# A fused linear attention and expert layer on one core: another order of work, six groups in flight instead of five

## What is computed

```
h    = layer_norm_over_channels(x)
q, k, v = h Wq + bq, h Wkv + bkv                  # 8 heads of 16
Q, K = elu(q) + 1, elu(k) + 1
out[l] = Q[l] . sum_{m<=l} K[m] v[m]^T / (Q[l] . sum_{m<=l} K[m])    # per head
x1   = x + out
t    = layer_norm_over_channels(x1)
probs = softmax(t gate_w + router_gamma), the two largest of 8 kept -> c[e]
y    = x1 + sum_e c[e] * (gam[e] * (t expert_w[e] + expert_b[e]) + bet[e])
```

## Time and profile before

| what | us |
|---|---|
| median of 3 runs (lowest, highest) | 998.53 (997.16, 1003.74) |
| the profiled execution, its own time | 1006.48 |
| span of that execution, first to last instruction | 1004.8 |
| PE busy | 832.0 |
| DVE busy | 766.5 |
| ACT busy | 440.0 |
| POOL busy | 405.4 |

### The profile page before, as it was taken

How to read it: one execution, slowest core, us unless ns; L and a number is a source line. 1 busy time by engine, 2 the same in 40 slices (tenths; PEclk the granted TensorE clock), 3 DMA queues, 4 the chain that set the end, 5 groups by cost and what they waited for, 6 DMA issues and landing times.

```text
span 1004.8 us, 25364 instructions
## 1 busy us (share of the span) xinstructions
PE 832.0 (83%) x8137; PEld 689.0 (69%) x8137; DVE 766.5 (76%) x2550; ACT 440.0 (44%) x1297; POOL 405.4 (40%) x639
## 2 busy tenths in 40 slices
PE   4678888888988889888888888888888898888885
PEld 2556667776777677766777777776667776767764
DVE  4677777778778887887877787778787778788764
ACT  1234444444444444444444444444444444444333
POOL 3254334434344444344443443344444334444311
PEclk9789888989889998999988998899998989898888
DMA  3000000000000000000000000000000000000000
GB/s 90 11 12 1 22 23 22 23 21 21 21 21 21 21 21 21 21 21 21 21 13 8 21 21 21 21 21 21 21 21 21 21 21 21 21 23 11 12 12 21
DMA packets 41200, 20.76 MB, mean 21 GB/s; under 512 B 1584, under 2 KB 41168, under 8 KB 41168
## 3 DMA queue, kind: packets, MB, share of 16 engines
q1 hardware_dynamic: 41168, 20.35, 7.5%
HBM read 10.90 MB, written 9.44 MB: 20 GB/s over the span
## 4 chain that ended last, share of the span: by engine, by line
PE 43%; DVE 33%; issue 14%; ACT 7%; DVEq 1%; POOL 1%; DMA 0%; SPq 0%; ACTq 0%; POOLq 0%
PE big L833 8%; DVE probs L540 6%; PE bank_n L845 6%; PE bank_n L887 5%; PE big L865 4%; DVE hot L614 4%; DVE y_dve L652 4%; PE bank_n L947 4%; ACT y_act L371 3%; DVE qkv L547 3%; DVE bn L527 3%; PE big L867 3%; PE big L866 3%; DVE o L670 2%; PE bank_q L906 2%
## 5 line engine op out<-in xcount | busy, mean ns | idle before, releaser
L540 DVE TENSOR_TENSOR probs<-big,tri 128x512 f32<-128x512 f32 x288 | 195.9, 681 | 75.6 <-PE big L833 75.6
L371 ACT ACTIVATE y_act<-big,scale 128x128 f32<-128x128 f32 x576 | 163.7, 374 | 0.0
L285 POOL TENSOR_TENSOR ve<-mv,eps 128x4 f32<-128x4 f32 x72 | 14.7, 204 | 318.4 <-DVE mv L532 318.3
L865 PE MATMUL big<-e_high,x_high 128*128 128x512 f32 x288 | 130.9, 455 | 10.5 <-DVE probs L540 4.9
L833 PE MATMUL big<-q_t,k_even 32*128 32x128 f32 x1152 | 75.2, 333 | 69.5 <-DVE y_dve L652 66.8
L833 PEld LDWEIGHTS big<-q_t,k_even 32*128 32x128 f32 x1152 | 54.1, 217 | 92.1 <-issue 89.8
L866 PE MATMUL big<-e_low,x_high 128*128 128x512 f32 x288 | 114.2, 396 | 0.0
L867 PE MATMUL big<-e_high,x_low 128*128 128x512 f32 x288 | 114.1, 396 | 0.0
L547 DVE SCALAR_TENSOR_TENSOR qkv<-bank_p,rstd,b_qkv 128x384 f32<-128x384 f32 x72 | 44.1, 613 | 72.0 <-PE bank_p L854 72.0
L652 DVE SCALAR_TENSOR_TENSOR y_dve<-big,scale,y_dve 128x128 f32<-128x128 f32 x288 | 87.1, 344 | 2.5
L652 DVE SCALAR_TENSOR_TENSOR y_dve<-big,scale,y_one 128x128 f32<-128x128 f32 x144 | 49.1, 345 | 46.7 <-ACT y_one L366 46.7
(11 more groups left out here) (150 smaller groups left out, 2086.9 us busy)
## 6 DMA issues: line engine op xcount, KB each, us to landing
x<-in_x SPq DMA_DIRECT2D x36, 256.0 KB, 3.0
out<-o SPq DMA_DIRECT2D x36, 256.0 KB, 2.3
beta_raw<-in_L_ffn_beta_w SPq DMA_DIRECT2D x1, 512.0 KB
e_raw<-in_L_ffn_expert_w SPq DMA_DIRECT2D x1, 512.0 KB
w_raw<-in_L_conv_Wkv SPq DMA_DIRECT2D x2, 64.0 KB, 2.3
b_qkv<-in_L_conv_bkv SPq DMA_DIRECT2D x1, 128.0 KB, 4.7
w_raw<-in_L_conv_Wq SPq DMA_DIRECT2D x1, 64.0 KB, 2.6
b_qkv<-in_L_conv_bq SPq DMA_DIRECT2D x1, 64.0 KB, 3.6
```

The costliest lines, as they stand in the source:

```text
L371: last = nc.scalar.activation(y_act[:, c.par, u, e], big[2 * s][:, 128 * e:128 * e + 128], ACT.Copy, scale=scale[:, c.par, u, e:e + 1])
L540: tt(probs[:, half, g].rearrange("p u e t -> p (u e) t"), big[g][:].rearrange("p (n t) -> p n t", t=T), tri[:].unsqueeze(1).broadcast_to([ ...
L865: mm(big[bank][:], x1_high[:, c.par, u], e_high[:, w], start=True, stop=False)
```

## The change

Every engine's step is written anew. The arithmetic, the shapes and the number of PE, DVE and POOL operations for one group stay as they are; one copy on ACT goes.

- **Stages.** A step now has six groups in flight, `g[0]` to `g[5]`: in step k, `g[n]` is group k - n. The steps run from k = 0 to 40, 41 in all. g[0] is the load and the transpose of x, g[1] its statistics' second part and low part, g[2] the projections and features, g[3] the sums of k, the transposes of k and q, the second half of the scores and the new state, g[4] the first half of the scores, attention, x1 and the first part of the routing, g[5] the rest of the routing, the experts, the output and the store.
- **Order.** The operations of different stages are interleaved in a new order on every engine, written out by hand in `step(k, g)`.
- **PSUM.** The banks have no owners. `AT`, `PROJ_AT`, `SCORES_AT` and `EXPERTS_AT` say in which of the eight banks each product stands; a bank serves three or four of them in turn within a step. The two halves of a unit's experts are apart in the order, and both halves of unit 2 stand in bank 1, one after the other.
- **Semaphores.** Each operation has its own, which counts groups, so that every wait is "n + 1" or near it.
- **x_res.** ACT's copy is gone. SP loads the same part of x from HBM a second time, into `x_res`, two steps before it is added.
- **The rest.** `y_one` has four buffers instead of two. The products of the remaining weights (`rest_of_weights`), which stood behind the first projections, now stand ahead of them, at the start of step 2, with a wait for the DVE operations that read them.

The diff is long (it writes all the step functions anew), so here are the constants, the order of stages, SP, and the start of PE's step; where the rest of the order matters, rows of it are shown below.

```diff
+REST_PSUM = 2 + 6 + EXPERTS + 1
+LAGS = 6
+REST_STEP = 2
+AT = dict(x=4, kv=3, att=6, x1_a=6, x1_b=4, k=1, q=7, coef=0, out=1)
+PROJ_AT = (4, 0, 3, 2)
+SCORES_AT = ((3, 7, 2, 0), (0, 5, 6, 7))
+EXPERTS_AT = ((4, 2), (6, 5), (1, 1), (2, 3))
...
-        y_one = sb("y_one", [128, 2, 128])
+        y_one = sb("y_one", [128, U, 128])
...
-            first, last = 2, CHUNKS - 2
-            for k in range(-2, PAR * first):
-                step(grp(k + 2), grp(k + 1), grp(k), grp(k - 1), grp(k - 2))
...
+            first = (LAGS + PAR) // PAR + 1
+            for k in range(PAR * first):
+                step(k, [grp(k - n) for n in range(LAGS)])
+            with eng.Fori(first, CHUNKS) as t:
+                for j in range(PAR):
+                    step(None, [Group(moved(t, (j - n) // PAR), (j - n) % PAR) for n in range(LAGS)])
+            for k in range(GROUPS, GROUPS + LAGS - 1):
+                step(k, [grp(k - n) for n in range(LAGS)])
...
+                if g[0]:
+                    n, p = g[0].i, g[0].par
+                    need(sp, "x_turned", n - 1)
+                    need(sp, "x_low", n - 1)
+                    if k != 0:
+                        sp.dma_start(x[:, p], dram(x_d, p, at[0])).then_inc(x_loaded[p], 16)
+                if g[5]:
+                    n, p = g[5].i, g[5].par
+                    need(sp, "out", n + 1)
+                    sp.dma_start(dram(out_d, p, at[5]), o[:, p]).then_inc(stored[p], 16)
+                if g[2]:
+                    n, p = g[2].i, g[2].par
+                    need(sp, "x1", n - 1)
+                    sp.dma_start(x_res[:, p], dram(x_d, p, at[2])).then_inc(x_res_loaded[p], 16)
...
-                    nc.scalar.activation(x_res[:, a.par], x[:, a.par], ACT.Copy).then_inc(S["x_res_done"], 1)
...
+            def step(k, g):
+                if k == REST_STEP:
+                    rest_of_weights()
+                    pe.wait_ge(S["rest_dve"], REST_PSUM)
+                if k == REST_STEP + 1:
                     pe.wait_ge(S["rest_dve"], REST_DVE)
```

More of the change, by code:

```diff
@@ L47 @@
 REST_DVE = 2 + 6 + EXPERTS + 2 + 4
[L48 to L56, removed]
+REST_PSUM = 2 + 6 + EXPERTS + 1
[5 more added lines that the diff above has]
+EXPERTS_AT = ((4, 2), (6, 5), (1, 1), (2, 3))
+WEIGHTS_AT = (0, 1, 2, 3)
+FIRST_AT = WEIGHTS_AT[0]
 class Group:
@@ L168, in program @@
         o = sb("o", [128, PAR, U, T])
[L170 to L183, removed]
+        bank = [ps(f"bank{n}") for n in range(8)]
@@ L192, in need @@
         def need(eng, name, count):
[L194 removed]
+            if not isinstance(count, int):
                 eng.wait_ge(S[name], count)
[L197 to L198 removed]
+            elif count > 0:
+                eng.wait_ge(S[name], min(count, GROUPS))
         def steps(eng, step):
@@ new lines, in turn_x, with project, turn_k @@
+            def turn_x(p):
+                for u in range(U):
+                    last = transpose(x_units[u], x[:, p, u], ident[:])
+                return last
+            def project(p, u):
+                out = bank[PROJ_AT[u]][:, 0:384]
+                mm(out, x_high[:, p, u], w_high[:], start=True, stop=False)
+                mm(out, x_high[:, p, u], w_low[:], start=False, stop=False)
+                return mm(out, x_low[:, p, u], w_high[:], start=False, stop=True)
+            def turn_k(p):
+                for u in range(U):
+                    last = transpose(bank[AT["k"]][:, T * u:T * u + T], feat[:, p, u, 128:256], ident[:])
+                return last
@@ L827, in scores, with turn_q @@
+            def turn_q():
+                for u in range(U):
+                    last = transpose(bank[AT["q"]][:, T * u:T * u + T], qn[:, u], ident[:])
+                return last
+            def scores(p, half):
                 for v in range(HALF_U):
@@ new lines, in values, with key_values @@
+                        for i in range(PAIRS):
+                            last = mm(bank[AT["att"]][32 * i:32 * i + 32, T * u:T * u + T], v_pad[:, p, u, 2 * i + e],
+                                      probs[:, half, i, v, e], start=False, stop=(e == 1), skip_group_check=True)
+                return last
+            def key_values(p):
+                for u in range(U):
+                    last = mm(bank[AT["kv"]][:, 128 * u:128 * u + 128], feat[:, p, u, 128:256], qkv[:, p, u, 256:384],
+                              start=True, stop=True)
+                return last
```

1197 lines of the change are left out of this document (633 added, 564 removed), and 9 rows, old and new, of the table names.

## The result

The changed kernel takes 755.89 us (median of 4 runs, 753.64 to 757.29); the kernel before took 999.72 us beside it (4 runs, 997.16 to 1003.74). The ratio is 0.7556, with a 95% interval of 0.7524 to 0.7589.

The account below looks back on a forecast made before the run. PE and DVE wait for each other in alternation, neither full; the new order would give 20.8 us a step. 154 + 31 x 20.8 + 1.7 = 800.5 us, times 0.992, gives 794 us; range 761 to 835, with rivals to 875.

Parts of the forecast that it names:

- its hold: DVE's sum of two masks, held until POOL's `qk` ended, 1175 ns on average; the new order would save 0.99 us.
- the sum: Whole span: start and end 66 + 88 = 154, plus 31 x 20.8, gives 799 us; with 1.7 around it, 800.5.
- The circle: Engines' new orders laid side by side from PE's last output transposes: a step closes at about 20 us.
- the four places called tight: Four places without slack in the new step: 0.4 us allowed, up to 26 us a step if all cost.
- What is left, 26.16 - 4.4 - 1.5 = 20.2 us, is PE's own work at full clock: PE's step before, 26.16 us, less 4.4 of waits and 1.5 of slow clock, leaves 20.2 us of work.
- the 0.6 us put on top: Added to each step: 0.2 us for short holds behind POOL's first `k_sum` operations, 0.4 for places without slack.
- DVE's 19.85 us: DVE's work in a new step: 20.84 us busy before, less 0.99 for the freed sum of two masks.
- The factor of 0.992: Median over profiled time of the kernel before, 998.53 against 1006.48 us, applied to 800.5 to give 794 us.
- Rival 1: Places without slack cost more, about half of DVE's idle time stays: 23.5 us a step, 881 us; chance 0.19.
- Rival 2: PE's clock falls in each step: 23.0 us a step, 864 us; chance 0.15.
- Rival 3: DVE operations with two SBUF inputs held behind POOL; eight such holds a step give 1044 us; chance 0.03.
- Rival 4: Late x loads or PE still waiting for projections keep a step at 26 to 27 us, about 980; chance 0.05.

Follow-up runs that it names:

- e7: The kernel before, with ACT's copy of x for the residual replaced by a second load from HBM: 1000.65 us, ratio 0.9989.
- e8: The changed kernel, loading only one of four images of x_res in whole steps: 755.7 us, ratio 0.7548.
- e3: The changed kernel without the third of three passes of each expert product on PE: 735.68 us, ratio 0.7395.
- e4: The changed kernel with DVE's sum of two masks, scale and coef moved behind `rden` and a bias, where POOL's `qn` runs: 804.94 us, ratio 0.8084.
- e12: The changed kernel with POOL adding four weighed expert outputs into two for units 1 and 2, and PE's unit 1 output transposes moved earlier: 741.85 us, ratio 0.7426.
- e5: The kernel before, with eight unread matmuls in PE's hole ahead of each step's first scores: 958.69 us, ratio 0.9583.

## Why the prediction was right and wrong

**Right.** The mechanism: two engines in turn became one full engine. Full clock in whole steps (1.00 in the window above; predicted over 0.97). The sum of the masks free of its hold (182 ns; predicted 190) and no wait of PE in a whole step. The second load at nothing (e7, e8); the semaphores and the `y_one` buffers too, in that PE has no idle time in whole steps that they could cause. The first whole step at 60 to 72 us: measured 68.78, where the sum had 66. The first scores of g[4] came at 49.51 (49 in the sum), but the step behind them took 19.27 us and not 17.9, with a wait for masks at its end:

```profile
68.78 0.61 PE L877 MATMUL bank<-q_t,k_even 32*128 32x128 f32 x8 [3.30 <-DVE probs L574]
```

The circle closed without a loss at any of the four places called tight, and x1 was made at 95.61, 6.1 us after the scores at 89.53, where 6.2 was worked out from the output's end.

**Right by luck.** The end: 88 us in the sum, 754.10 - 666.09 = 88.0 measured. Steps 36 and 37 took 18.9 and 18.8 us, not 20.8 each; the last two steps took 750.64 - 721.74 = 28.9 us up to the last residual, not 14 + 11 = 25. Two errors of 4 us cancel.

**Wrong: the size of a step, 20.8 us instead of 19.27.** Against the sum of 800.5 us, 31 x 20.8 - 597.3 = 47.5 us are missing; the later start gives back 2.8. The step that failed is "What is left, 26.16 - 4.4 - 1.5 = 20.2 us, is PE's own work at full clock", and with it the 0.6 us put on top. PE's own work is 19.22 us. It can be read by laying PE's starts in before's step beside those of the changed kernel. PE's own rows are not enough for it; the row PEld, the load of a matmul's weights, shows a wait that they hide. First before:

```profile
568.22 1.05 PE L947 MATMUL bank_n<-q_t,state 128*128 128x128 f32 x8
568.57 0.68 DVE L540 TENSOR_TENSOR probs<-big,tri 128x512 f32<-128x512 f32 x1
...
569.30 0.31 PEld L833 LDWEIGHTS big<-q_t,k_even 32*128 32x128 f32 x8 [0.23 <-DVE probs L540]
569.31 0.50 PE L833 MATMUL big<-q_t,k_even 32*128 32x128 f32 x8
```
```profile
578.00 0.60 PE L875 MATMUL bank_t<-ident,x 128*128 128x128 f32 x4
578.82 0.50 PE L865 MATMUL big<-e_high,x_high 128*128 128x512 f32 x1 [0.21 <-DVE probs L540]
```

Then the changed kernel:

```profile
437.65 1.05 PE L884 MATMUL bank<-q_t,state 128*128 128x128 f32 x8
438.46 0.42 PE L853 MATMUL bank<-w_high,x_high 128*128 128x384 f32 x1
...
441.86 0.34 PE L853 MATMUL bank<-w_high,x_high 128*128 128x384 f32 x1
...
442.92 1.09 PE L909 MATMUL bank<-id_gate,x 128*128 128x136 f32 x8
443.76 0.48 PE L915 MATMUL bank<-e_high,x_high 128*128 128x512 f32 x1
```

- Before's step has a fourth wait, at 578.82, that I did not subtract: 0.21 us and the 0.18 of the modelled end, 0.39 us. The four transposes of x ahead of it take 578.82 - 578.00 = 0.82 us there; in the changed kernel, without the wait, they take 0.44.
- Six projection passes take 442.92 - 441.86 = 1.06 us; I had set 2 x 0.63 against the slow ones: 0.20 us.
- The eight state products have the same modelled duration in both, 1.05 us, but what stands behind them starts 1.09 us after them in before and 438.46 - 437.65 = 0.81 here: 0.28 us. In before that is the second scores, and it is a fifth wait: the load of their weights waited 0.23 us for a mask of DVE's, which ended at 568.57 + 0.68 = 569.25. (Up to 0.10 us of the 0.28 may be the scores' own: behind an expert product of the changed kernel they start 450.13 - 449.80 = 0.33 us later, where the next expert product starts 0.23 later.)
- Eight transposes with the gate's columns take 443.76 - 442.92 = 0.84 us, where I took 0.94: 0.10 us.

These four make 0.97 of the 1.0 us, or a little less; 0.67 of it are two waits that the prediction left in what it called PE's own work, and 0.30 are matmuls that it took as slower than they are. The remedy would have been to add up PE's work kind by kind from its tightest place, not to subtract the listed waits from a period. The 0.6 us on top measured nothing: where PE has 576.49 of 576.56 us, the tight places of 30 steps together have cost no more than the 0.07 us that is left.

**Wrong too: DVE's 19.85 us**, which is 18.5. It made 20 us look like a floor from two sides ("the circle closes at about 20 us"). The timelines of DVE, first before, then after, show one reason:

```profile
516.52 0.18 DVE L575 TENSOR_TENSOR lg<-lg,router_b 128x32 f32<-128x32 f32 x1
516.73 0.19 DVE L578 TENSOR_REDUCE top<-lg 128x4 f32<-128x32 f32 x1
516.95 0.19 DVE L582 TENSOR_TENSOR lgm<-lg,top 128x32 f32<-128x32 f32 x1
517.18 0.19 DVE L587 SCALAR_TENSOR_TENSOR rank<-lgm,order 128x32 f32<-128x32 f32 x1
```
```profile
95.22 0.18 DVE L647 TENSOR_REDUCE top<-rank 128x4 f32<-128x32 f32 x1
95.31 0.18 DVE L649 TENSOR_TENSOR probs_e<-probs_e,rstd 128x32 f32<-128x32 f32 x1
95.41 0.18 DVE L653 TENSOR_SCALAR den<-den 128x32 f32<-128x32 f32 x1
95.49 0.19 DVE L657 TENSOR_TENSOR hot<-rank,top 128x32 f32<-128x32 f32 x1
95.61 0.69 DVE L664 TENSOR_TENSOR x<-bank,x_res 128x512 f32<-128x512 f32 x1
96.21 0.18 DVE L668 TENSOR_TENSOR hot<-hot 128x32 f32<-128x32 f32 x1
```

Each operation lasts 0.18 us in both. In before each needs the one ahead of it, and they start 0.21 to 0.23 us apart; in the new order operations of different chains alternate and start 0.09 to 0.12 us apart. The order cut DVE's busy time by more than the hold, which a sum over durations can't show. How much of the 1.35 us it makes was not measured by itself.

**Wrong, the other way: the factor of 0.992.** It came from one profiled execution of before, whose four other runs lie between 997 and 1004 us. The changed kernel's profiled run (755.91) is its median. The factor took off 6.5 us and so hid part of the error.

**The range.** All sizes of the step erred on one side. Its low end, 20.0 us "if all falls into place", was the same sum again and no bound; with 19.2 it would have held the time. The prediction also gave 140 to 170 us for start and end, and then took 145 and 158 in the range; with 140 the low end is 755.6 us, which would have held the time by luck, with the step still wrong.

**The rivals.** Rival 1 did not come: no repeated wait. Rival 2 neither: clock 1.00. The Trainium skill ("TensorE: Matmul & The Clock Gate", section "A second HAM failure mode: psum-queue depth-cycling") warns of a clock that swings from short idle times between banks; in e3 with 3% and in e4 with 374.35 of 400 us busy the clock stayed at 1.00, so these two runs don't bear it out. The kernel before, with PE busy for 85% of its whole steps and holes of up to 2 us, does swing. Rival 3's mechanism was shown by e4, but at no place of the new order; its rule ("SBUF — State Buffer", section "SBUF: two separate sides") agrees with the rows of e4, where each held operation ended 0.04 to 0.05 us behind POOL's. Rival 4 fell: a step has 19.22 us, and the waits of the whole steps list none for x or `x_res`.

## What to carry to other kernels

When two engines wait for each other, the gain of a new order is read from the own work of the one that will be full; add it up kind by kind, from start to start, at the tightest place in the trace, since a period minus its listed waits keeps the ones that the list misses, such as a wait of PEld's behind which PE's row shows none. Put small VectorE operations with two SBUF inputs where GpSimd has nothing to run, and let independent short chains alternate (the second was seen in the trace, not tested alone). Once one engine is at 100%, move work off it (e12), and look first at how close the next one is.

## What the runs showed of the hardware that was not expected

- Two operations in a row can be held (e4): POOL's next instruction had started before the second of two DVE operations that depend on each other. 0.36 us of work took 1.99.
- Unread matmuls made a kernel 4% faster (e5), with a mean clock of 0.968 instead of 0.906; the edit does nothing else but add work. A hole is not enough to lower it: in e5 PE stands still throughout 515 to 516 us, ahead of its fourth projection, and the clock stays at 1.00 there and behind. In the kernel before, the same hole (at 512 to 514) has 0.50 behind it, at 515.

```profile
515.00:516.00 1.00, 0.00 (x0) 0.00 (x0) 1.00 (x3) 0.26 (x2) 0.81 (x2) 1.00 0.00 0
516.00:517.00 1.00, 0.88 (x6) 0.88 (x7) 1.00 (x3) 0.64 (x1) 1.00 (x2) 1.00 0.00 0
```

- Small dependent operations on DVE start at half the rate of independent ones (0.21 to 0.23 us apart against 0.09 to 0.12).
